# A second gating cycle that takes two of the second layer's four tiles in three passes

## The chip, the cores and the metric

The kernel runs on one core of a Trainium2 chip. The metric is the device time of one execution in microseconds (us); lower is better. The engines that matter here are TensorE (PE, with its weight loads shown apart as PEld), VectorE (DVE), ScalarE (ACT), GpSimd (POOL) and SyncE (SP), which issues transfers. Each engine works through its own list of instructions in the order written; between engines there are semaphores.

## The reference

One block of a gated cross-attention network, for 4 sequences of 1024 tokens of width 512, in float32. First x + tanh(g) * attention(layernorm(x), ctx) with 16 heads, a mask and an added matrix. Then the part that the change touches:

```python
def _coupling_net(h, w1, b1, w2, b2, w3, b3, w4, b4):
    h = _gelu(h @ w1 + b1)      # 512 -> 512
    h = _gelu(h @ w2 + b2)      # 512 -> 256
    h = _gelu(h @ w3 + b3)      # 256 -> 128
    return jax.nn.sigmoid(h @ w4 + b4)   # 128 -> 1
...
out = x                          # x is the layernorm of the first part's result
for _ in range(3):
    tf = _coupling_net(out, ...)
    combined = 0.7 * gf + 0.3 * tf
    coupling = BASE_COUPLING + adaptive_range * (combined - 0.5) * 2.0
    out = out + coupling * _twist(out)
```

`_twist` swaps and negates the four quarters of a row, so after any number of cycles `out` is alpha * x + beta * twist(x) with two numbers alpha and beta per token. The first layer is linear before its bias, so the kernel computes A = x @ w1 and B = twist(x) @ w1 once, and each cycle's first layer is gelu(alpha * A + beta * B + b1), an element-wise mix.

## The kernel before

The kernel has three phases: projections (up to about 300 us), attention (to about 1286 us) and the feed-forward phase, in `ffn_phase`, from there to the end. The change lies in the last alone.

`ffn_phase` goes through 4 batches (one sequence each, some 120 us), every batch through two column blocks j = 0 and 1 of 512 tokens. A batch projects the attention's output, normalises, computes A and B (`first_layer`), and then runs CYCLES = 3 gating cycles n = 0, 1, 2 on each block; the loop counter is k = 2n + j. All arrays lie transposed: 128 partitions by 4 tiles (m or t = 0 to 3) of features, 512 tokens along each row. For each (n, j):

- DVE, `mix(b, n, j)` for n = 1 and 2: multiplies and adds A and B into the tiles u[j][:, m] (f_u). For n = 1 that is one multiplication and one addition a tile. `coefficients` ahead of it turns the gate (f_coef) into alpha and beta.
- ACT, `h1`: Gelu of a tile of u, in place. It then raises h1_ready.
- PE, `layer2`: for each tile t, two matmuls (one for each half of the 256 outputs) of w2[:, t] with u[j][:, t], accumulated in f_acc.
- ACT `h2_half` twice, PE `layer3` (two matmuls), ACT `h3_all`, PE `layer4` (one matmul), ACT `gate` (a tanh), then DVE again for the other cycle.

A matmul has two forms. In plain float32 it is one `pe.matmul`, which the trace shows as two records. In the other form both operands are split into a high part of reduced precision (fp32r) and the rest as a low part; `three_pass` multiplies high by high, low by high and high by low, three records of a line each (L164, L165, L166). Cycle n = 0 has this form for all four tiles: ACT writes a second Gelu with an fp32r output (u_hi) ahead of the float32 one, and DVE subtracts the two into u_lo (`split_u`, L1624), which lies in the same place as u. Cycles 1 and 2 use plain float32 (L1328).

The order of the work is written out by hand. On PE, around one k: `layer2(k, tiles 1 to 3)`, `layer3(k)`, `layer2(k + 1, tile 0)`, `layer4(k)`. On ACT, the Gelus of the following cycle's tiles for the other block lie between the steps of k: h2_half, h2_half, h1 of tile 0, h3_all, h1 of tile 1, gate, h1 of tiles 2 and 3. So the h1 of block j in cycle n stands in the step k of the other block just ahead.

Two transfers for the following batch wait for the last use of u_hi, since they land in its memory or beside it: SP's `load_x(b + 1, 1)` into f_x_rows1 and POOL's `load_attention(b + 1, 0, part)` into X_hi and X_lo. Both count z2_ready up to cycle SPLIT - 1, so to the end of the second layer of cycle 0.

Of the kernel before, what the change touches and what calls it, by code (L numbers as in the profile page):

```python
# [10 lines left out]
F32 = mybir.dt.float32  # L11
F32R = mybir.dt.float32r
I32 = mybir.dt.int32
ALU = mybir.AluOpType
# [976 lines left out]
def ffn_phase(nc, weighted, x_bo, x_bo_stored, small, ident, wo_hi, wo_lo, w1_raw, w1_loaded, X_hi, X_lo, X_loaded, x1, x_loaded,  # L991
# [1 line left out]
    NJ = S // CH  # L993
    F2, F3 = E // 2, E // 4
    CYCLES = 3
    SPLIT = 1
    GPB = H // HPG
    LATE = 2 * (B * GPB - 2)

# [5 lines left out]
    with ExitStack() as ctx:  # L1005
# [127 lines left out]
        def turn(b, n, j):  # L1133

            return (CYCLES * b + n) * NJ + j

        def turn_split(b, n, j):

            return (SPLIT * b + n) * NJ + j

        def coef_steps(b, n, j):

# [101 lines left out]
        def _(pe):  # L1244
# [62 lines left out]
            def layer2(b, n, j, tiles):  # L1307

                k = turn(b, n, j)
                if n == 0 and 0 in tiles:  # L1310
                    if j == 0:
                        pe.wait_ge(own_read, 2 * ET * NJ * (b + 1))
                    else:
                        pe.wait_ge(shared_read, 4 * ET * NJ * (b + 1))
                for t in tiles:
                    if n < SPLIT:
                        pe.wait_ge(w2_lo_ready, b + 1)
                        pe.wait_ge(u_lo_ready, ET * turn_split(b, n, j) + t + 1)
                        for m in range(2):
                            ms = slice(m * P, (m + 1) * P)  # L1320
                            last = three_pass(pe, acc[:, 2 * j + m, :], w2_hi[:, t, ms], w2_lo[:, t, ms], u_hi[j][:, t, :], u_lo[j][:, t, :],
                                              t == 0, t == ET - 1)
                            if t == ET - 1:
                                last.then_inc(z2_ready, 1)
                        continue
                    pe.wait_ge(h1_ready, ET * k + t + 1)
                    for m in range(2):
                        last = pe.matmul(acc[:, 2 * j + m, :], w2[:, t, m * P:(m + 1) * P], u[j][:, t, :], start=t == 0, stop=t == ET - 1)  # L1328
                        if t == ET - 1:
                            last.then_inc(z2_ready, 1)  # L1330
# [75 lines left out]
        def _(act):  # L1406
# [51 lines left out]
            def h1(b, n, j, m):  # L1458
                k = ((CYCLES - 1) * b + n - 1) * NJ + j
                act.wait_ge(u_ready, ET * k + m + 1)  # L1460
                if n < SPLIT:
                    act.activation(u_hi[j][:, m, :], u[j][:, m, :], ACT.Gelu, bias=small.b1[:, m:m + 1])
                act.activation(u[j][:, m, :], u[j][:, m, :], ACT.Gelu, bias=small.b1[:, m:m + 1]).then_inc(h1_ready, 1)  # L1463

# [96 lines left out]
        def _(dve):  # L1561
# [55 lines left out]
            def split_w2(b):  # L1617
                dve.wait_ge(w2_hi_ready, b + 1)
                dve.tensor_tensor(w2_lo[:], w2[:], w2_hi[:].bitcast(F32), ALU.subtract).then_inc(w2_lo_ready, 1)

            def split_u(b, n, j):
                for m in range(ET):
                    dve.wait_ge(h1_ready, ET * turn(b, n, j) + m + 1)
                    dve.tensor_tensor(u_lo[j][:, m, :], u[j][:, m, :], u_hi[j][:, m, :].bitcast(F32), ALU.subtract).then_inc(u_lo_ready, 1)  # L1624

            def coefficients(b, n, j):

# [15 lines left out]
            def mix(b, n, j):  # L1643

                k = ET * (((CYCLES - 1) * b + n - 1) * NJ + j)
                dve.wait_ge(coef_step, coef_steps(b, n - 1, j))

                def multiply(m):
                    if n == 1:
                        dve.tensor_tensor(u[j][:, m, :], Bt[j][:, m, :], beta[:, j, :], ALU.mult).then_inc(mul_ready, 1)  # L1650
                    else:
                        dve.tensor_tensor(u[j][:, m, :], A[j][:, m, :], alpha[:, j, :], ALU.mult).then_inc(mul_ready, 1)
                        dve.tensor_tensor(Bt[j][:, m, :], Bt[j][:, m, :], beta[:, j, :], ALU.mult).then_inc(B_scaled, 1)

                def add(m):
                    dve.wait_ge(mul_ready, k + m + 1)
                    if n == 2:
                        dve.wait_ge(B_scaled, ET * (NJ * b + j) + m + 1)
                    other = A if n == 1 else Bt
                    dve.tensor_tensor(u[j][:, m, :], u[j][:, m, :], other[j][:, m, :], ALU.add).then_inc(u_ready, 1)  # L1660

                multiply(0)
                for m in range(1, ET):
                    multiply(m)
                    add(m - 1)
                add(ET - 1)

            def gated_columns(b, j):
# [45 lines left out]
            def batch(b, first, more):  # L1714
# [39 lines left out]
                for k in range(NJ * CYCLES):  # L1754
                    n, j = k // NJ, k % NJ
                    if n < CYCLES - 1:
                        coefficients(b, n, j)
                        mix(b, n + 1, j)
                        if n + 1 < SPLIT:
                            split_u(b, n + 1, j)  # L1760
                    else:
                        gated_columns(b, j)
                        y_columns(b, j)
                        if j == 0:
                            for s in range(TT):
                                finish(b, 0, s)
# [87 lines left out]
```

## Time and profile before

| what | value |
|---|---|
| median of 3 runs | 1780.76 us (1780.32 to 1783.08) |
| the profiled execution: its time | 1781.25 us |
| the profiled execution: its span | 1779.5 us |
| PE busy | 1744.4 us, 98% |
| DVE busy | 1467.6 us, 82% |
| ACT busy | 1250.7 us, 70% |
| POOL busy | 658.9 us, 37% |
| mean granted clock of TensorE | 0.994 |

The span runs from the first instruction to the last; the execution's own time holds 1.75 us more. In rows of the trace a start is in us from the span's start, and "x12" says that the row merges 12 like records. A record's duration on PE, DVE or ACT is longer than the distance to the next start, because instructions overlap in the pipeline: what an engine spends on one is read from the distance between starts.

### The profile page before, as it was taken

The page shows a single profiled execution, that of the slowest core. Times are in us where ns is not written, and L with a number is a line of the kernel's source. Part 1 is how long each engine was busy: PE and PEld are TensorE (multiplying, and loading weights), DVE is VectorE, ACT ScalarE, POOL GpSimd, SP SyncE. Part 2 cuts the span into 40 slices and gives each one's busy share as a digit, 9 for nine tenths or more (in the row PEclk, how much of TensorE's full clock was granted, in tenths as well). Part 3 has the DMA queues.
Part 4 walks back from the last instruction along what each step waited for, and adds up shares of the span by engine and source line. Part 5 has one row for each costly group of instructions (what it writes and reads, how often), then busy time and mean ns, then how long its engine had stood idle before and what let it go on. Part 6 is the DMA issues. An engine that isn't in the chain of part 4 may idle for free. (4 is left out here: it accounts for less than half of the span.)

```text
span 1779.5 us, 34050 instructions
## 1 busy us (share of the span) xinstructions
PE 1744.4 (98%) x12392; PEld 1290.0 (72%) x12392; DVE 1467.6 (82%) x2554; ACT 1250.7 (70%) x2185; POOL 658.9 (37%) x591
## 2 busy tenths in 40 slices
PE   7999999999999999999999999999999999999997
PEld 6888887777777777777777777777676585674873
DVE  5544545999999999999999999999777976877868
ACT  3232324999999999999999999999764365465455
POOL 3342342323278542487432695353325010010100
PEclk9999999999999999999999999999999999999999
DMA  7778675756367665377753676744512614212101
GB/s 266 254 247 287 230 265 153 181 159 144 107 170 202 125 145 120 106 215 159 145 134 85 185 190 125 159 97 114 158 51 71 192 48 118 86 54 66 63 1 48
DMA packets 152214, 254.63 MB, mean 143 GB/s; under 512 B 17024, under 2 KB 69504, under 8 KB 152064
## 3 DMA queue, kind: packets, MB, share of 16 engines
q1 hardware_dynamic: 101408, 157.73, 27.5%
q0 software_dynamic: 50080, 93.87, 23.8%
q8 instruction: 92, 1.51, 0.4%
q10 hardware_dynamic: 576, 1.05, 0.2%
q14 instruction: 58, 0.48, 0.1%
HBM read 168.44 MB, written 84.15 MB: 142 GB/s over the span
## 5 line engine op out<-in xcount | busy, mean ns | idle before, releaser
L967 DVE CUSTOM_DVE_ANT_0 a_neg<-a_sc_ps,am 128x1024 f32<-128x1024 f32 x512 | 620.9, 1213 | 1.3 <-PE a_sc_ps L820 1.3
L916 ACT ACTIVATE a_prob<-a_neg,a_row_min 128x1024 f32<-128x1024 f32 x512 | 586.0, 1144 | 7.7 <-DVE a_row_min L967 4.6
L832 PEld LDWEIGHTS a_tr_ps<-ident,a_prob 128*128 128x128 f32 x4096 | 460.3, 140 | 136.2 <-issue 100.3
L832 PE MATMUL a_tr_ps<-ident,a_prob 128*128 128x128 f32 x4096 | 545.8, 276 | 1.4 <-ACT a_probT L896 1.4
L942 DVE COPY a_probT<-a_tr_ps 128x512 f32<-128x512 f32 x512 | 353.8, 691 | 49.0 <-PE a_tr_ps L832 36.5
L896 ACT ACTIVATE a_probT<-a_tr_ps 128x512 f32<-128x512 f32 x512 | 305.6, 597 | 74.3 <-PE a_tr_ps L832 49.2
L716 POOL DMA_DIRECT2D a_q_st<-q_parts x144 | 79.6, 559 | 211.7 <-PE a_sc_ps L820 176.6
L853 PE MATMUL a_o_ps<-a_probT,v_first 128*32 128x256 f32 x2048 | 137.0, 385 | 0.0
L853 PE MATMUL a_o_ps<-a_probT,a_v 128*32 128x256 f32 x2048 | 136.4, 385 | 0.2 <-ACT a_probT L896 0.2
L1328 PE MATMUL f_acc<-f_u,f_w 128*128 128x512 f32 x256 | 115.9, 595 | 0.4 <-ACT f_u L1463 0.3
L820 PE MATMUL a_sc_ps<-k_first,a_q_st 96*128 96x512 f32 x384 | 113.7, 417 | 0.0
L820 PE MATMUL a_sc_ps<-a_k_st,a_q_st 96*128 96x512 f32 x384 | 113.1, 416 | 0.0
L916 ACT ACTIVATION_READ_ACCUMULATOR a_prob<-a_neg,a_row_min 128x1 f32 x512 | 97.0, 190 | 0.0
L721 POOL TENSOR_SCALAR a_m_raw<-a_m_raw 128x1024 f32<-128x1024 int32 x24 | 86.9, 3630 | 25.6 <-DMA a_m_raw<-mask 25.4
L1328 PEld LDWEIGHTS f_acc<-f_u,f_w 128*128 128x128 f32 x256 | 47.6, 190 | 61.4 <-issue 48.3
L853 PEld LDWEIGHTS a_o_ps<-a_probT,a_v 128*32 128x32 f32 x2048 | 53.7, 109 | 43.6 <-issue 20.6
L853 PEld LDWEIGHTS a_o_ps<-a_probT,v_first 128*32 128x32 f32 x2048 | 53.4, 109 | 43.3 <-issue 21.3
L132 POOL TENSOR_TENSOR st_o<-st_o,st_rinv 128x512 f32<-128x512 f32 x32 | 41.4, 1294 | 111.0 <-DMA st_rinv<-rinv_all 110.9
L820 PEld LDWEIGHTS a_sc_ps<-k_first,a_q_st 96*128 96x128 f32 x384 | 64.8, 189 | 9.4 <-DVE a_row_min L967 1.2
L820 PEld LDWEIGHTS a_sc_ps<-a_k_st,a_q_st 96*128 96x128 f32 x384 | 65.1, 189 | 8.5
L1222 POOL TENSOR_TENSOR f_rstd<-f_var_eps,f_minus_half 128x4 f32<-128x4 f32 x8 | 10.4, 1298 | 161.6 <-DVE f_neg_mean L1592 161.6
L463 DVE SCALAR_TENSOR_TENSOR p_out_lo<-p_acc,p_bias_k,p_out_hi 128x512 fp32r<-128x512 f32 x32 | 23.7, 749 | 55.1 <-ACT p_out_hi L395 55.1
(221 smaller groups left out, 3109.7 us busy)
## 6 DMA issues: line engine op xcount, KB each, us to landing
a_q_st<-q_parts POOLq DMA_DIRECT2D x144, 128.0 KB, 2.9
k_first<-k_parts POOLq DMA_DIRECT2D x24, 512.0 KB, 8.2
a_k_st<-k_parts POOLq DMA_DIRECT2D x24, 512.0 KB, 7.5
a_m_raw<-mask SPq DMA_DIRECT2D x24, 512.0 KB, 4.9
a_adj_raw<-adj SPq DMA_DIRECT2D x24, 512.0 KB, 6.1
p_x_raw<-x POOLq DMA_DIRECT2D x8, 1024.0 KB, 8.0
k_parts<-p_out_hi SPq DMA_DIRECT2D x32, 256.0 KB, 3.0
k_parts<-p_out_lo SPq DMA_DIRECT2D x32, 256.0 KB, 6.2
```

The lines of the kernel that those rows point to most:

```text
L132: pool.tensor_tensor(w.o[:], w.o[:], w.rinv[:], ALU.mult).then_inc(w.step, 1)
L463: dve.scalar_tensor_tensor(out_lo[:, m, :], acc[:, (n0 + m) % 4, :], bias[:, m:m + 1], out_hi[:, m, :].bitcast(F32), ALU.add, ALU.subtract ...
L716: pool.dma_start(q_st[qb][quad * D:(quad + 1) * D], src).then_inc(q_loaded[qb], 16)
L721: pool.tensor_scalar(m_raw[:, t % 2, :].bitcast(F32), m_raw[:, t % 2, :], 0.0, -BIG, ALU.is_equal, ALU.mult).then_inc(big_ready, 1)
L820: last = pe.matmul(sc_ps[:, r % 2, half * 512:(half + 1) * 512], q_st[qb][0:STACK, h, qt * P:(qt + 1) * P], k_st[par][0:STACK, h, half * 5 ...
L832: last = pe.transpose(tr_ps[:, half, j * P:(j + 1) * P], prob[:, r % NPROB, t * P:(t + 1) * P], ident[:])
L853: last = pe.matmul(o_ps[h * D:(h + 1) * D, prev % 2, 0:QB], v_sb[vpar][:, t, h * D:(h + 1) * D], probT[:, prev % 2, h, t, :], start=(t == ...
L896: act.activation(probT[:, (r // UB) % 2, h, 0:4, qt * P:(qt + 1) * P], tr_ps[:, 0, :].rearrange("p (t q) -> p t q", t=4), ACT.Copy).then_i ...
L916: act.activation(prob[:, r % NPROB, :], neg[:, r % 2, :], ACT.Exp, scale=-1.0, bias=row_min[:, r % 2:r % 2 + 1], accum_out=row_sum[:, r // ...
L942: dve.tensor_copy(probT[:, (r // UB) % 2, h, 4:8, qt * P:(qt + 1) * P], tr_ps[:, 1, :].rearrange("p (t q) -> p t q", t=4)).then_inc(tr_rea ...
L967: dve.tensor_tensor_reduce(out=neg[:, r % 2, :], in0=sc_ps[:, r % 2, :], in1=am[:, 2 * qb + qt, :], scale=-1.0, scalar=3.4e38, op0=ALU.add ...
L1328: last = pe.matmul(acc[:, 2 * j + m, :], w2[:, t, m * P:(m + 1) * P], u[j][:, t, :], start=t == 0, stop=t == ET - 1)
```

## The change

The second gating cycle (n = 1) takes its tiles 0 and 1 in three passes; tiles 2 and 3 stay float32. ACT's `h1` writes u_hi too for those two. DVE subtracts inside `mix`: the subtraction for tile 0 after the addition of tile 1, that for tile 1 after the addition of tile 2. SPLIT is 2 now, so the two transfers wait for the second layer of cycle 1.

```diff
-    SPLIT = 1
+    SPLIT = 2
+    PARTS = (4, 2)
...
-        def turn_split(b, n, j):
+        def parts_before(b, n, j):
 
-            return (SPLIT * b + n) * NJ + j
+            return NJ * sum(PARTS) * b + NJ * sum(PARTS[:n]) + PARTS[n] * j
...
                 for t in tiles:
-                    if n < SPLIT:
+                    if n < SPLIT and t < PARTS[n]:
                         pe.wait_ge(w2_lo_ready, b + 1)
-                        pe.wait_ge(u_lo_ready, ET * turn_split(b, n, j) + t + 1)
+                        pe.wait_ge(u_lo_ready, parts_before(b, n, j) + t + 1)
...
                 act.wait_ge(u_ready, ET * k + m + 1)
-                if n < SPLIT:
+                if n < SPLIT and m < PARTS[n]:
                     act.activation(u_hi[j][:, m, :], u[j][:, m, :], ACT.Gelu, bias=small.b1[:, m:m + 1])
...
+            def split_u_tile(b, n, j, m):
+                dve.wait_ge(h1_ready, ET * turn(b, n, j) + m + 1)
+                dve.tensor_tensor(u_lo[j][:, m, :], u[j][:, m, :], u_hi[j][:, m, :].bitcast(F32), ALU.subtract).then_inc(u_lo_ready, 1)
+
             def split_u(b, n, j):
-                for m in range(ET):
...
+                for m in range(PARTS[n]):
+                    split_u_tile(b, n, j, m)
...
                 for m in range(1, ET):
                     multiply(m)
                     add(m - 1)
+                    if n == 1 and m >= 2:
+                        split_u_tile(b, 1, j, m - 2)
                 add(ET - 1)
...
                         mix(b, n + 1, j)
-                        if n + 1 < SPLIT:
-                            split_u(b, n + 1, j)
```

On DVE, in the first batch, the mixing of block 0 for cycle 1 (f_u_18572 is u of block 0, f_u_lo_18574 and f_u_hi_18560 its low and high parts). Before:

```order
L1650 TENSOR_TENSOR f_u_18572<-f_B_18570,f_beta 128x512 [waits f_coef_step]
L1650 TENSOR_TENSOR f_u_18572<-f_B_18570,f_beta 128x512
L1660 TENSOR_TENSOR f_u_18572<-f_u_18572,f_A_18569 128x512 [waits f_mul_ready]
L1650 TENSOR_TENSOR f_u_18572<-f_B_18570,f_beta 128x512
L1660 TENSOR_TENSOR f_u_18572<-f_u_18572,f_A_18569 128x512 [waits f_mul_ready]
L1650 TENSOR_TENSOR f_u_18572<-f_B_18570,f_beta 128x512
L1660 TENSOR_TENSOR f_u_18572<-f_u_18572,f_A_18569 128x512 [waits f_mul_ready] x2
```

The same place on DVE in the changed kernel (its lines are numbered four on):

```order
L1654 TENSOR_TENSOR f_u_18572<-f_B_18570,f_beta 128x512 [waits f_coef_step]
L1654 TENSOR_TENSOR f_u_18572<-f_B_18570,f_beta 128x512
L1664 TENSOR_TENSOR f_u_18572<-f_u_18572,f_A_18569 128x512 [waits f_mul_ready]
L1654 TENSOR_TENSOR f_u_18572<-f_B_18570,f_beta 128x512
L1664 TENSOR_TENSOR f_u_18572<-f_u_18572,f_A_18569 128x512 [waits f_mul_ready]
L1624 TENSOR_TENSOR f_u_lo_18574<-f_u_18572,f_u_hi_18560 128x512 [waits f_h1_ready]
L1654 TENSOR_TENSOR f_u_18572<-f_B_18570,f_beta 128x512
L1664 TENSOR_TENSOR f_u_18572<-f_u_18572,f_A_18569 128x512 [waits f_mul_ready]
L1624 TENSOR_TENSOR f_u_lo_18574<-f_u_18572,f_u_hi_18560 128x512 [waits f_h1_ready]
L1664 TENSOR_TENSOR f_u_18572<-f_u_18572,f_A_18569 128x512 [waits f_mul_ready]
```

The two subtractions (L1624) are new; the last multiplication and the last two additions stand behind one or both of them.

On ACT, the same stretch: the step of cycle 0, block 1, with the Gelus of cycle 1, block 0 in it. Before:

```order
L1467 ACTIVATE f_h_1_18577<-f_acc,small_b_71 128x512 [waits f_z2_ready] x2
L1463 ACTIVATE f_u_18572<-f_u_18572,small_b_70 128x512 [waits f_u_ready]
L1471 ACTIVATE f_h_1_18577<-f_tr,small_b_72 128x512 [waits f_z3_ready]
L1463 ACTIVATE f_u_18572<-f_u_18572,small_b_70 128x512 [waits f_u_ready]
L1476 ACTIVATE f_coef<-f_z,small_half_b_75 128x512 [waits f_z4_ready]
L1463 ACTIVATE f_u_18572<-f_u_18572,small_b_70 128x512 [waits f_u_ready] x2
```

The same place on ACT in the changed kernel:

```order
L1468 ACTIVATE f_h_1_18577<-f_acc,small_b_71 128x512 [waits f_z2_ready] x2
L1463 ACTIVATE f_u_hi_18560<-f_u_18572,small_b_70 128x512 [waits f_u_ready]
L1464 ACTIVATE f_u_18572<-f_u_18572,small_b_70 128x512
L1472 ACTIVATE f_h_1_18577<-f_tr,small_b_72 128x512 [waits f_z3_ready]
L1463 ACTIVATE f_u_hi_18560<-f_u_18572,small_b_70 128x512 [waits f_u_ready]
L1464 ACTIVATE f_u_18572<-f_u_18572,small_b_70 128x512
L1477 ACTIVATE f_coef<-f_z,small_half_b_75 128x512 [waits f_z4_ready]
L1464 ACTIVATE f_u_18572<-f_u_18572,small_b_70 128x512 [waits f_u_ready] x2
```

A Gelu into f_u_hi stands ahead of the plain one for tiles 0 and 1; both still stand behind the two h2 halves.

## Rows read from the trace of the kernel before

**Rows 1.** The page, part 1: busy time, share of the span, instructions.
```profile
PE 1744.4 (98%) x12392; PEld 1290.0 (72%) x12392; DVE 1467.6 (82%) x2554; ACT 1250.7 (70%) x2185; POOL 658.9 (37%) x591
```
**Rows 2.** Chain of waits, second batch: start, us, engine, what, line.
```profile
1489.46 1.72 PE f_acc L1328 x4
...
1529.63 1.04 PE f_tr L1350 x8
```
**Rows 3.** Timeline of PE, second batch: start, us, engine, line, operation, out<-in, count.
```profile
1489.30 1.88 PE L1328 MATMUL f_acc<-f_u,f_w 128*128 128x512 f32 x4
1491.01 1.02 PE L1344 MATMUL f_z<-f_h,small_w 128*128 128x512 f32 x2
1491.87 5.31 PE L1328 MATMUL f_acc<-f_u,f_w 128*128 128x512 f32 x12
...
1498.92 1.88 PE L1328 MATMUL f_acc<-f_u,f_w 128*128 128x512 f32 x4
```
**Rows 4.** Timeline of ACT, second batch; in brackets idle time and its releaser.
```profile
1486.73 1.37 ACT L1467 ACTIVATE f_h<-f_acc,small_b 128x512 f32<-128x512 f32 x2 [2.75 <-PE f_acc L166]
1488.00 0.71 ACT L1463 ACTIVATE f_u<-f_u,small_b 128x512 f32<-128x512 f32 x1
1489.50 0.69 ACT L1471 ACTIVATE f_h<-f_tr,small_b 128x512 f32<-128x512 f32 x1 [0.79 <-PE f_tr L1336]
...
1492.66 1.32 ACT L1463 ACTIVATE f_u<-f_u,small_b 128x512 f32<-128x512 f32 x2
...
1497.81 0.71 ACT L1463 ACTIVATE f_u<-f_u,small_b 128x512 f32<-128x512 f32 x1
```
**Rows 5.** Timeline of DVE, second batch.
```profile
1485.81 0.68 DVE L1660 TENSOR_TENSOR f_u<-f_u,f_A 128x512 f32<-128x512 f32 x1
...
1502.42 0.55 DVE L1636 TENSOR_SCALAR f_coef<-f_coef,small_range,f_base 128x512 f32<-128x512 f32 x1 [4.14 <-ACT f_coef L1476]
```
**Rows 6.** Chain of waits, second batch: PE released by a subtraction of DVE.
```profile
1433.76 0.70 DVE X_lo L1604
1434.50 0.50 PE f_acc L164
```
**Rows 7.** Timeline of PE, second batch: two records of an unbroken three-pass stretch, then one behind rows 6.
```profile
1410.03 0.40 PE L166 MATMUL f_acc<-wo_lo,X_hi 128*128 128x512 f32 x1
...
1428.43 0.39 PE L166 MATMUL f_acc<-wo_lo,X_hi 128*128 128x512 f32 x1
...
1434.84 0.39 PE L165 MATMUL f_acc<-X_hi,f_w_lo 128*128 128x512 f32 x1
```
**Rows 8.** Timeline of PE's weight loads, second batch.
```profile
1493.42 0.36 PEld L1328 LDWEIGHTS f_acc<-f_u,f_w 128*128 128x128 f32 x2 [0.50 <-ACT f_u L1463]
```
**Rows 9.** Timeline of ACT, first batch.
```profile
1366.89 0.72 ACT L1463 ACTIVATE f_u<-f_u,small_b 128x512 f32<-128x512 f32 x1 [0.69 <-DVE f_u L1660]
```
**Rows 10.** Timeline of DVE, first batch.
```profile
1377.90 1.75 DVE L1660 TENSOR_TENSOR f_u<-f_u,w_raw 128x512 f32<-128x512 f32 x1
```
**Rows 11.** Timeline of POOL, first batch.
```profile
1377.50 1.60 POOL L141 TENSOR_TENSOR st_lo<-st_o,st_hi 128x512 f32<-128x512 f32 x1
```
**Rows 12.** Timeline of PE, first batch.
```profile
1369.48 1.02 PE L1344 MATMUL f_z<-f_h,small_w 128*128 128x512 f32 x2
...
1379.11 1.02 PE L1344 MATMUL f_z<-f_h,small_w 128*128 128x512 f32 x2
1380.46 5.42 PE L1328 MATMUL f_acc<-f_u,f_w 128*128 128x512 f32 x12 [0.33 <-ACT f_u L1463]
```
**Rows 13.** Stretches: us, busy of PE, PEld, DVE, ACT, POOL (x instructions), PEclk (granted clock), DMA, GB/s.
```profile
1350.00:1380.00 30.00, 27.75 (x85) 15.16 (x83) 24.08 (x27) 12.39 (x21) 17.75 (x15) 1.00 0.23 71
...
1460.00:1479.00 19.00, 18.92 (x81) 15.20 (x80) 13.52 (x22) 9.76 (x19) 1.56 (x2) 0.94 0.24 67
```
**Rows 14.** Timeline of POOL, second batch: a transfer is issued for the following one.
```profile
1487.67 0.74 POOL L1205 DMA_DIRECT2D X_hi<-att_parts  x1 [12.58 <-PE f_acc L166]
```
**Rows 15.** Issues of transfers: out<-in, queue, count, KB each, median us from issue to landing.
```profile
X_lo<-att_parts POOLq DMA_DIRECT2D x6, 1024.0 KB, 8.4
```

More of the change, by code:

```diff
@@ L1619, in split_w2 @@
                 dve.tensor_tensor(w2_lo[:], w2[:], w2_hi[:].bitcast(F32), ALU.subtract).then_inc(w2_lo_ready, 1)
+            def split_u_tile(b, n, j, m):
+                dve.wait_ge(h1_ready, ET * turn(b, n, j) + m + 1)
+                dve.tensor_tensor(u_lo[j][:, m, :], u[j][:, m, :], u_hi[j][:, m, :].bitcast(F32), ALU.subtract).then_inc(u_lo_ready, 1)
             def split_u(b, n, j):
-                for m in range(ET):
-                    dve.wait_ge(h1_ready, ET * turn(b, n, j) + m + 1)
-                    dve.tensor_tensor(u_lo[j][:, m, :], u[j][:, m, :], u_hi[j][:, m, :].bitcast(F32), ALU.subtract).then_inc(u_lo_ready, 1)
+                for m in range(PARTS[n]):
+                    split_u_tile(b, n, j, m)
             def coefficients(b, n, j):
```

## The prediction

> **What bounds the kernel now.** I read the busy shares first: PE is busy 98% of the span [rows 1], so what PE spends counts unless something makes it wait. Then the chain of waits, which shows whose waits set the end: in the gating cycles of the second batch every link from 1489.46 to 1529.63 is a matmul [rows 2], and the third and fourth batches repeat that pattern. Last the timelines of that stretch, engine by engine, since the change adds links between engines to a chain that holds only PE. A full PE there does not say that the others have room: it says that they are just in time, and how closely is the question.
>
> **What PE saves.** A float32 matmul takes 0.86 us: the four records of tile 0 start at 1489.30 and layer 4 follows at 1491.01, and layer 4, one matmul, ends as tile 1 starts at 1491.87 [rows 3]. In a three-pass stretch 81 records lie between the starts 1410.03 and 1428.43, 0.227 us each [rows 7], so 0.68 us a matmul. A tile is two matmuls: 1.72 before, 1.36 after, 0.36 saved. There are 4 batches x 2 blocks x 2 tiles: 16 x 0.36 = 5.8 us, if nothing waits.
>
> **What ACT and DVE add.** ACT gets 16 Gelus at a distance of 0.61 us (two in 1.32, one in 0.71 [rows 4]). DVE gets 16 subtractions with two inputs in SBUF, as the additions have, 0.68 long at a distance of about 0.60 (I take the addition's 0.68 [rows 5]). By amount both fit: DVE stands idle 4.14 us ahead of the coefficients of cycle 1 [rows 5]. By place they don't.
>
> **Tile 0, block 0 (k = 2).** The mixed tile is ready at 1485.81 + 0.68 = 1486.49 [rows 5], but ACT's first Gelu on it stands behind the two h2 halves and starts at 1488.00 [rows 4]. Before, it ended at 1488.71 and PE started tile 0 at 1489.30 with 0.59 in hand [rows 3]. Now the high part comes first, the plain one starts 0.61 later and ends at 1489.32. Only then can DVE subtract, 1489.35 to 1490.03; its queue holds nothing else until then, since three multiplications and two additions are through. PE's start behind a subtraction: the one that ended at 1434.46 let PE go at 1434.50, and the next record stood at 1434.84 instead of one distance later, so the steady pace began at 1434.61, 0.15 behind DVE's end [rows 6, 7]. Tile 0 thus runs at pace from 1490.18 and ends at 1491.54, against 1491.01 before. Stall 0.88, saving 0.36 (with rounding): layer 4 is 0.53 late. h3_all, at 1489.50 before [rows 4], is not late, since ACT is free at 1489.22.
>
> **Tile 1.** ACT goes h3_all, high part 1490.09, plain 1490.7 to 1491.4; DVE, having done the last multiplication and the third addition, subtracts 1491.43 to 1492.11. PE wants tile 1 when layer 4 is through, at 1491.87 + 0.53 = 1492.40: no stall, with about 0.1 to spare for the weights. The fourth addition, behind that subtraction, ends at 1492.7, in time for ACT's last Gelu. PE is through tile 1 at 1493.77.
>
> **Tile 2, where the second saving goes.** Its Gelu stands behind the gate, which waits for layer 4. Before, it started at 1492.66 and ended at about 1493.37; the weight load of tile 2 waited for it until 1493.42 [rows 4, 8], only 0.17 ahead of PE's turn at 1491.87 + 1.72 = 1493.59. This chain (layer 4, gate, Gelu, load) is measured from layer 4, not from tile 1. A tile 1 that is 0.36 shorter leaves PE waiting 0.36 longer: tile 2 starts 0.53 late, as layer 4 was. So the saving of tile 1 is nothing, and k = 2 ends 0.53 late.
>
> **Block 1 (k = 3).** The same, with one difference: the second h2 half comes later there, so the Gelu of tile 0 starts 1.11 ahead of PE's turn (1497.81, 1498.92 [rows 3, 4]) instead of 1.30 (1488.00, 1489.30). Plain Gelu to 1499.13, subtraction to 1499.84, pace from 1499.99, end 1501.35 against 1498.92 + 1.72 = 1500.64: 0.71 more. Tile 1's saving goes as before. Together 0.53 + 0.71 = 1.24 us a batch.
>
> **Cycle 2.** Its mixing starts when the gate of k = 2's step has come, 1502.42 [rows 5]; DVE waits for it, so it moves by the same 1.24, and so do ACT and PE behind it. Nothing is won back: cycle 2 had no PE stall to absorb. Three batches: 3.7 us.
>
> **The first batch.** GpSimd is still at work on the attention's output there, and DVE is late. At k = 2 the first Gelu starts at 1366.89 [rows 9], so the plain one ends at 1368.2, the subtraction at 1368.93, tile 0 at 1368.93 + 0.15 + 1.36 = 1370.44 against 1369.48 [rows 12]: 0.97. At k = 3 DVE's mixing before is slowed to one operation of 1.75 us for each of GpSimd's of 1.60 [rows 10, 11], until GpSimd ends at 1379.10; the addition of tile 1 ends at 1379.65, and the new subtraction of tile 0 stands behind it. DVE's start is 0.97 later there, but what it gets is one operation behind each GpSimd one, so I let that addition end where it did: subtraction 1379.6 to 1380.3, tile 0 at pace from 1380.4 to 1381.8, layer 4 to 1382.6, tile 1 to 1384.0, tile 2 (0.48 + 0.61 + 0.61 + about 0.05 behind layer 4) at 1384.3. Before, tile 1 started at 1380.46, already 0.33 late [rows 12], and tile 2 at 1382.28. That makes 2.1 us for this batch, and 1.2 if the mixing weren't slowed, 3.8 if it lost one slot of 1.75.
> The Trainium skill (SBUF — State Buffer, section "SBUF: two separate sides") has the shared port pair as an exclusive lock held for a whole instruction. That agrees with the 1.75 beside 1.60 [rows 10, 11]. By it the late start is swallowed, as I assume; by a proportional slowdown the mixing would keep its 0.97 and this batch would cost up to 0.9 more.
>
> **Transfers.** POOL issued the part for the next batch at 1487.67, at the end of the second layer of cycle 0, and the median to landing is 8.4 us [rows 14, 15]. Now it waits for cycle 1's, near 1508, and lands near 1518; PE needs it at 1530.7 [rows 2]. SP's load of f_x_rows1 moves to about 1498 and is needed later still. Behind POOL's waiting issue stands nothing before the next batch, behind SP's the store of y(b, 0), which isn't ready until 1530. Cost nothing; without that cover project would start late by the whole lack.
>
> **Sum.** 3.7 + 2.1 = 5.8 us. On the profiled execution's 1781.25 (span 1779.5 and 1.75 around it) that is 1787.1; that execution is 0.5 over the median of 1780.76, which the forecast starts from: 1786.6 us, slower by 0.33%. From both sides: the new wait of PE on DVE is measured on one row, 0.15; between 0 and 0.35 it moves the sum by -1.2 to +1.6. The first batch gives -0.9 to +1.7. Its own range is 1784.5 to 1789.
>
> **Rivals.**
> First, PE's saving counts and the waits don't: low parts are there when PE comes. Then 5.8 us come off: 1775.0. It decides at tile 0: the subtraction would have to end before 1489.2, 0.8 earlier than I find, so ACT would have to begin at 1487.2, while it is on the h2 halves from 1486.73 [rows 4]. For it speaks only that tile 0 was mixed 1.5 us before its Gelu. 7%.
> Second, tile 2 isn't tied to layer 4: the load row [rows 8] was merely the load's own turn, and tile 1's 0.36 is kept. Then a batch costs 0.53, the first about 1.4, together 3.0: 1783.8, within what a measurement can tell from no change (0.2%, 3.6 us). Against it, the row names ACT's Gelu as the releaser, 0.05 behind its end. 13%.
> Third, the clock. PE gets eight more gaps of 0.9 to 2.4 us. The granted clock fell to 0.94 over 19 us with PE busy 18.92, some 1.1 us, and stayed at 1.00 over 30 us with 2.25 idle [rows 13]. If each gap brought such a fall (stretches at 1.2 GHz between those at 2.4), 8 x 1.1 = 9: 1796. 8%.
> The Trainium skill speaks for it (TensorE: Matmul & The Clock Gate, section "A second HAM failure mode: psum-queue depth-cycling"): frequent short idles between groups of matmuls make the clock swing. The 1.00 over 2.25 us of idle [rows 13] is against that here.
> That the change doesn't do what it says is no rival: the orders of DVE and ACT show the new instructions where they should stand.
>
> **Chances.** The forecast 72%, so slower by over 0.2% (the forecast and the clock) 80%, within 0.2% 13%, faster 7%. Range: 1782 to 1790 takes in the second rival and the bounds of the first batch; outside lie the first and third (15%) and a little of the forecast's edges.
>
> **What would show it.** Right: in cycle 1 PE idles some 0.9 to 1.1 us ahead of L164 on f_u_hi, released by DVE's f_u_lo, eight times (over 2 once in the first batch), and 0.3 to 0.4 ahead of the first L1328 behind, released by ACT's f_u; batches two to four are 1.2 us longer. Wrong: no idle behind tile 1, project waiting for X_hi, or a granted clock under 0.98 between 1480 and 1530.

## The result and the profile after

The changed kernel takes 1788.6 us (median of 9 runs, 1785.08 to 1794.89) against 1782.17 us for the kernel before, run beside it (median of 9, 1780.32 to 1783.36). The ratio is 1.0041, with a 95% interval of 1.0032 to 1.0050: slower by 7.3 us (5.7 to 8.9). The forecast was 5.8 us more and 1786.6 us, with a range of 1782 to 1790. The profiled execution took 1789.46 us with a span of 1787.7 us, 8.2 us over the span before.

The page's first part after, with the same columns as [rows 1]:

```profile
PE 1745.3 (98%) x12424; PEld 1297.1 (73%) x12424; DVE 1477.2 (83%) x2570; ACT 1260.3 (71%) x2201; POOL 658.5 (37%) x591
```

PE's share of busy time reads 98% before and after, and its busy time even rose by 0.9 us, although the new matmuls are the shorter ones. The loss shows only in what isn't busy: span less busy time is 35.1 us before and 42.4 us after. ACT and DVE show their 16 new instructions each, 9.6 us.

The timeline of PE in the second batch shows it. Columns are start, us, engine, line, operation, operands, count; in brackets the idle time ahead and its releaser. Line 1337 is layer 3, 1345 layer 4, 1329 the float32 matmul:

```profile
1490.03 1.98 PE L1337 MATMUL f_tr<-f_h,f_w 128*128 128x512 f32 x4
1492.74 0.47 PE L164 MATMUL f_acc<-f_u_hi,f_w_hi 128*128 128x512 f32 x1 [0.73 <-DVE f_u_lo L1624]
...
1494.19 1.02 PE L1345 MATMUL f_z<-f_h,small_w 128*128 128x512 f32 x2
...
1496.60 3.70 PE L1329 MATMUL f_acc<-f_u,f_w 128*128 128x512 f32 x8
1500.21 1.98 PE L1337 MATMUL f_tr<-f_h,f_w 128*128 128x512 f32 x4
1503.11 0.47 PE L164 MATMUL f_acc<-f_u_hi,f_w_hi 128*128 128x512 f32 x1 [0.91 <-DVE f_u_lo L1624]
...
1504.55 1.02 PE L1345 MATMUL f_z<-f_h,small_w 128*128 128x512 f32 x2
```

Before, this stretch ran without a gap [rows 3]. The bracketed 0.73 is counted from the modelled end of layer 3's last record; from layer 3's start at 1490.03 tile 0 used to begin 1.83 us later, at 1491.86, so its first record is 0.88 late.

ACT and DVE at the same place, the rows that answer to [rows 4, 5]:

```profile
1489.29 1.37 ACT L1468 ACTIVATE f_h<-f_acc,small_b 128x512 f32<-128x512 f32 x2 [2.75 <-PE f_acc L166]
1490.55 0.71 ACT L1463 ACTIVATE f_u_hi<-f_u,small_b 128x512 fp32r<-128x512 f32 x1
1491.16 0.71 ACT L1464 ACTIVATE f_u<-f_u,small_b 128x512 f32<-128x512 f32 x1
```

```profile
1489.56 0.69 DVE L1664 TENSOR_TENSOR f_u<-f_u,f_A 128x512 f32<-128x512 f32 x1
1491.90 0.69 DVE L1624 TENSOR_TENSOR f_u_lo<-f_u,f_u_hi 128x512 fp32r<-128x512 f32 x1 [1.66 <-ACT f_u L1464]
```

The plain Gelu ends at 1491.87, DVE subtracts from 1491.90 to 1492.59, and PE starts at 1492.74. PE's next record stands at 1493.05, so it is at pace from 1492.82, 0.23 behind DVE's end and 0.96 late; the forecast had 0.15 and 0.88, from [rows 6, 7]. DVE idled 1.66 us: nothing else in its order could go ahead of the subtraction.

The weight loads of PE ahead of tile 2, the row that answers to [rows 8]:

```profile
1496.59 0.30 PEld L1329 LDWEIGHTS f_acc<-f_u,f_w 128*128 128x128 f32 x2 [0.44 <-ACT f_u L1464]
```

PE's last record of tile 1 starts at 1496.19 and is through at pace at 1496.42, so this load at 1496.59 has nothing left to hide behind. Before, it ran under a matmul.

Most readings below use one distance, taken from PE's timelines: from the start of layer 3 at k = 1 (cycle 0, block 1) to the first layer-4 matmul in columns of the last cycle, which spans everything the change touches in one batch. In us, from one profile each:

| kernel | first batch | second | third | fourth |
|---|---|---|---|---|
| before | 34.11 | 33.26 | 33.27 | 33.25 |
| changed | 35.90 | 34.61 | 34.63 | 34.65 |
| difference | +1.79 | +1.35 | +1.36 | +1.40 |

The four differences make 5.9 us. The rest of the 8.2 us lies outside that stretch, where the two kernels have the same instructions, and is the granted clock, less 0.9 us by which the phase began earlier. The stretches here have the columns of [rows 13]:

```profile
1462.00:1466.00 4.00, 4.00 (x12) 3.20 (x11) 1.23 (x1) 1.51 (x3) 0.00 (x0) 0.59 0.00 0
...
1702.00:1706.00 4.00, 4.00 (x23) 3.57 (x23) 2.21 (x5) 1.93 (x4) 0.00 (x0) 0.78 0.02 6
1706.00:1710.00 4.00, 4.00 (x16) 3.17 (x15) 1.48 (x2) 1.65 (x3) 0.00 (x0) 0.79 0.00 0
```

Each such fall costs about 1.6 us: from the last cycle to layer 3 of the next batch's k = 1 the profiles have 86.2 us or 87.8 us and nothing between. The kernel before had one of these (87.79 between its first and second batch), the changed one two (87.75 and 87.79), and one more in its first batch, between 1334 and 1340. These falls stand in the first layer, before the change's part of the batch, and follow 16 matmuls with one column of output; they are not where the new gaps are.

### The profile page after: what moved, and what is told of

Same layout as the page of the kernel before. It is cut to its first block and busy times, and to the rows that moved or that the text cites. A ratio compares the mean times of both kernels' runs of the same rounds, so it can differ in the third digit from the quotient of the medians.

```text
span 1787.7 us, 34162 instructions
## 1 busy us (share of the span) xinstructions
PE 1745.3 (98%) x12424; PEld 1297.1 (73%) x12424; DVE 1477.2 (83%) x2570; ACT 1260.3 (71%) x2201; POOL 658.5 (37%) x591
## 5 line engine op out<-in xcount | busy, mean ns | idle before, releaser
L1329 PE MATMUL f_acc<-f_u,f_w 128*128 128x512 f32 x192 | 87.9, 600 | 0.0
L1616 DVE TENSOR_TENSOR f_B<-f_B,f_acc 128x512 f32<-128x512 f32 x64 | 43.7, 683 | 31.6 <-PE f_acc L166 21.7
L380 ACT ACTIVATE p_c_hi<-p_c_raw 128x2048 fp32r<-128x2048 f32 x7 | 13.4, 1919 | 78.3 <-PE p_acc L166 50.4
```

## The experiments

All ratios are against the kernel before, run on the same chip in the same rounds; microseconds over or under before are the ratio's distance from 1, times 1782.

**Tile 0 alone.** In cycle 1 only tile 0 is taken in three passes.

```diff
-    PARTS = (4, 2)
+    PARTS = (4, 1)
...
-                    if n == 1 and m >= 2:
+                    if n == 1 and m == 2:
```

> Only tile 0 of cycle 1 is taken in three passes; tile 1 is float32 again, without its second Gelu and subtraction. Theory (the wait behind layer 4, gate and Gelu fixes when tile 2 starts, so tile 1's saving is worth nothing): as the changed kernel, 5.8 us over before (5.5 to 6.2), and no idle of PE ahead of tile 2. Rival (tile 1's saving of 0.36 counts, eight times): 2.9 us slower than the changed kernel, 8.7 over before.

Measured: 1787.4 us, ratio 1.0035 (1.0023 to 1.0048), 6.2 us over before. By distance a batch costs 34.70, 34.69 and 34.70 in the second to fourth, +1.43; the changed kernel +1.37. So tile 1's three passes, which are 0.36 us shorter, bring 0.06 a batch. Its first batch had 35.37 in this profile. In the trace layer 4 and what follows it are the same:

```profile
1489.76 0.47 PE L164 MATMUL f_acc<-f_u_hi,f_w_hi 128*128 128x512 f32 x1 [0.73 <-DVE f_u_lo L1624]
...
1491.21 1.02 PE L1345 MATMUL f_z<-f_h,small_w 128*128 128x512 f32 x2
1492.06 5.31 PE L1329 MATMUL f_acc<-f_u,f_w 128*128 128x512 f32 x12
1497.29 1.99 PE L1337 MATMUL f_tr<-f_h,f_w 128*128 128x512 f32 x4
```

From layer 4 to the next layer 3 it takes 6.08 us here with a float32 tile 1, and 1500.21 - 1494.19 = 6.02 us in the changed kernel with the shorter one. The saving of tile 1 is turned into the wait for tile 2, as the forecast had it; the rival that counted it is out.

**Late transfers alone.** The kernel before with the two waits for the next batch's transfers one cycle later.

```diff
-                            sp.wait_ge(z2_ready, 2 * turn(b, SPLIT - 1, 0) + 2)
+                            sp.wait_ge(z2_ready, 2 * turn(b, SPLIT, 0) + 2)
...
-                    pool.wait_ge(z2_ready, 2 * turn(b - 1, SPLIT - 1, 1) + 2)
+                    pool.wait_ge(z2_ready, 2 * turn(b - 1, SPLIT, 1) + 2)
```

> The kernel before, with only the two waits for transfers moved to the end of the second layer of cycle 1, as in the changed kernel. Theory (they are covered): 0 us, within 0.5. Rival (late transfers are the 1.5 us by which the changed kernel is over the forecast): +1.5 us.

Measured: 1781.35 us, ratio 0.9990 (0.9982 to 0.9999). The transfers are covered. In the changed kernel POOL issues at 1510.96 what it issued at 1487.67 before [rows 14], and PE needs it some 23 us later. The interval ends just under 1; its three later batches are 33.26, 33.25 and 33.26, as before. Its first batch had 33.25 where the kernel before had 34.11; further down such differences turn out to go with GpSimd's place.

**High passes first.** The changed kernel, but PE waits in cycle 1 for the high part only, does the four passes that read it, and then waits for the low part.

```diff
                     if n < SPLIT and t < PARTS[n]:
                         pe.wait_ge(w2_lo_ready, b + 1)
+                        if n == 1:
+                            pe.wait_ge(u_hi_ready, 2 * (NJ * b + j) + t + 1)
+                            for m in range(2):
+                                ms = slice(m * P, (m + 1) * P)
+                                pe.matmul(acc[:, 2 * j + m, :], w2_hi[:, t, ms], u_hi[j][:, t, :], start=t == 0, stop=False)
+                                pe.matmul(acc[:, 2 * j + m, :], w2_lo[:, t, ms], u_hi[j][:, t, :], start=False, stop=False)
+                            pe.wait_ge(u_lo_ready, parts_before(b, n, j) + t + 1)
+                            for m in range(2):
+                                pe.matmul(acc[:, 2 * j + m, :], w2_hi[:, t, m * P:(m + 1) * P], u_lo[j][:, t, :], start=False, stop=False)
+                            continue
...
-                    act.activation(u_hi[j][:, m, :], u[j][:, m, :], ACT.Gelu, bias=small.b1[:, m:m + 1])
+                    act.activation(u_hi[j][:, m, :], u[j][:, m, :], ACT.Gelu, bias=small.b1[:, m:m + 1]).then_inc(u_hi_ready, 1)
```

> The changed kernel, but in cycle 1 PE waits for the high part alone, does the four passes of a tile that read it, and only then waits for the low part and does the other two. Theory (the loss is PE's wait on the low part): that wait is covered by 4 x 0.227 = 0.91 us of passes; tile 0 then ends 0.36 earlier than in float32 on block 0 and 0.2 on block 1, 0.56 a batch in batches two to four, and in the first batch, where DVE's subtraction stands behind an addition held up by GpSimd, about 1.2 late: together -0.5 us against before (-1.5 to +0.5), 6 under the changed kernel. Rival (the added work on ACT and DVE costs by itself, wherever PE waits): no more than 1 us under the changed kernel.

Measured: 1781.37 us, ratio 0.9995 (0.9987 to 1.0004): 8 us under the changed kernel, with the same 16 Gelus and 16 subtractions. The batches are 32.71, 32.72 and 32.72, which is -0.55 each against the -0.56 worked out; the first is 36.12, +2.0 instead of +1.2, and it holds a fall of the clock (granted 0.50 from 1383 to 1386) behind 1.79 us in which PE idled. The wait is gone from the timeline:

```profile
1490.60 1.98 PE L1348 MATMUL f_tr<-f_h,f_w 128*128 128x512 f32 x4
1492.02 0.79 PE L1324 MATMUL f_acc<-f_u_hi,f_w_hi 128*128 128x512 f32 x1
...
1493.35 0.62 PE L1328 MATMUL f_acc<-f_u_lo,f_w_hi 128*128 128x512 f32 x2
1493.81 1.02 PE L1356 MATMUL f_z<-f_h,small_w 128*128 128x512 f32 x2
```

Layer 4 begins 3.21 us behind layer 3's start; 3.54 before, 4.16 in the changed kernel. The loss was the wait on the low part, not the work that makes it.

**Gelu of tile 2 ahead of the gate.** The changed kernel with one ACT instruction moved, in the step of cycle 0, block 1.

```diff
+                    if k == 1:
+                        h1(*other, 2)
                     if n < CYCLES - 1:
                         gate(b, n, j)
...
                     if between:
-                        h1(*other, 2)
+                        if k != 1:
+                            h1(*other, 2)
```

> The changed kernel, but in the step of cycle 0, block 1, ACT does the Gelu of tile 2 ahead of the gate instead of behind it. Theory (tile 2 waits on layer 4, gate, Gelu): PE's idle ahead of tile 2 of block 0 goes, 0.36 four times, 1.4 us under the changed kernel, 4.4 over before. Rival (that idle isn't there, or is made good by the next wait): as the changed kernel.

Measured: 1790.73 us, ratio 1.0041 (1.0029 to 1.0054), as the changed kernel. The whole time says no, the trace says yes and why. From layer 3 of k = 1 to that of k = 2 it is 9.94, 9.92 and 9.94 us in the three later batches against 10.18 in the changed kernel, 0.25 less where 0.36 was expected, and the load of tile 2 waits for nobody:

```profile
1499.62 0.19 PEld L166 LDWEIGHTS f_acc<-f_u_lo,f_w_hi 128*128 128x128 f32 x1
1499.85 0.42 PEld L1329 LDWEIGHTS f_acc<-f_u,f_w 128*128 128x128 f32 x2
```

The first batch takes it back: 37.52 us, where the changed kernel's profile had 35.90. PE idles 2.45 us ahead of tile 0 of block 1 there, and the granted clock is 0.50 from 1383 to 1386. The same gap was 2.18 us long in the changed kernel's profile, and no fall followed it. The moved Gelu needn't be the cause of the fall: the kernel with the first batch alone, further down, has the same one without it.

**The second Gelu alone.** The kernel before with late transfers, and ACT's Gelu into u_hi for tiles 0 and 1 of cycle 1, which nobody reads. DVE and PE are untouched.

```diff
-                if n < SPLIT:
+                if n == 1 and m < 2:
                     act.activation(u_hi[j][:, m, :], u[j][:, m, :], ACT.Gelu, bias=small.b1[:, m:m + 1])
```

> The kernel before with the later transfers and, in cycle 1, ACT's second Gelu for tiles 0 and 1, whose result nobody reads; DVE and PE work as before. Theory (what counts is how far tile 0's plain Gelu is from PE's turn, not ACT's idle time): PE waits 0.2 us more at tile 0 of block 0 and 0.4 at that of block 1, 0.6 a batch and about 1.0 in the first, together 2.8 us over before (2.0 to 3.5), near half of the changed kernel's loss. Rival (ACT is 70% busy, so 16 Gelus fit): 0 us.

Measured: 1784.5 us, ratio 1.0008 (0.9993 to 1.0022). The interval can't tell the theory from the rival, but the distances can: 33.80 in all four batches, +0.54 in the second to fourth (0.6 expected). The first has 33.80 too, where the kernel before had 34.11 in its profile; the 1.0 expected there didn't come. So 1.6 us of the later batches' 4.1 come with ACT's instruction alone, though ACT was busy only 70% of the span: in its order the plain Gelu moves 0.61 back.

**The passes alone.** The kernel before with late transfers; in cycle 1 PE takes tiles 0 and 1 in three passes, all on the high part left from cycle 0. The low part of cycle 1 is left out.

```diff
                     pe.wait_ge(h1_ready, ET * k + t + 1)
+                    if n == 1 and t < 2:
+                        for m in range(2):
+                            ms = slice(m * P, (m + 1) * P)
+                            three_pass(pe, acc[:, 2 * j + m, :], w2_hi[:, t, ms], w2_lo[:, t, ms], u_hi[j][:, t, :], u_hi[j][:, t, :], t == 0, False)
+                        continue
```

> The kernel before with the later transfers, and in cycle 1 PE takes tiles 0 and 1 in three passes, all three on the high part that cycle 0 left, waiting for the plain Gelu alone; ACT and DVE do nothing new. The low part of cycle 1 is left out. Theory: tile 0 gives its 0.36 us on both blocks, tile 1's is lost behind layer 4, gate and Gelu: 0.72 a batch, none in the first, where DVE is the limit: 2.2 us under before (1.5 to 2.8). Rival (all 32 matmuls' saving counts): 5.8 us under before.

Measured: 1779.33 us, ratio 0.9986 (0.9971 to 1.0002), 2.5 us under before where 2.2 was expected and the rival had 5.8; the interval excludes a gain of 5.8. The distances are 32.54 three times, -0.72 each, the figure worked out to the second digit. The first batch has 35.07, so nothing was gained there. Even with ACT and DVE spared, half of what PE saves is lost behind layer 4, gate and Gelu.

**The changed kernel again.**

> The changed kernel once more, beside the others on one chip. Theory (5.9 us of waits, and the rest of the 7.3 measured is the clock's scatter): 5.9 us over before at the same granted clock. Rival (the new gaps bring clock falls): a mean granted clock at least 0.001 under that of the kernel before, and 7.3 us or more.

Measured: 1790.95 us (12 runs, 1787.77 to 1793.94), ratio 1.0047 (1.0032 to 1.0062), 8.4 us. Its mean granted clock is 0.9916, against 0.9931 for 34 of the 35 executions of the kernel before beside it. The one left out (1796.13 us, clock 0.960) stands 12 us above all others; with it the mean is 0.9922, and the rival's condition on the clock isn't met. So the means point to the clock but don't settle it. The profile shows a place: its later batches are 34.65, 34.64 and 34.64, but the first takes 40.44 us, 6.3 more than before. PE there:

```profile
1363.93 1.98 PE L1337 MATMUL f_tr<-f_h,f_w 128*128 128x512 f32 x4
1369.51 0.77 PE L164 MATMUL f_acc<-f_u_hi,f_w_hi 128*128 128x512 f32 x1 [3.60 <-DVE f_u_lo L1624]
...
1372.21 1.91 PE L1345 MATMUL f_z<-f_h,small_w 128*128 128x512 f32 x2
```

DVE, and then POOL:

```profile
1364.74 1.75 DVE L1664 TENSOR_TENSOR f_u<-f_u,f_A 128x512 f32<-128x512 f32 x1
1366.41 1.75 DVE L1654 TENSOR_TENSOR f_u<-f_B,f_beta 128x512 f32<-128x512 f32 x1
1368.09 0.68 DVE L1664 TENSOR_TENSOR f_u<-f_u,f_A 128x512 f32<-128x512 f32 x1
1368.69 0.68 DVE L1624 TENSOR_TENSOR f_u_lo<-f_u,f_u_hi 128x512 fp32r<-128x512 f32 x1
```

```profile
1362.68 1.59 POOL L137 TENSOR_TENSOR st_hi<-st_lo,st_o 128x512 f32<-128x512 f32 x1
1364.35 1.59 POOL L139 TENSOR_TENSOR st_hi<-st_lo,st_hi 128x512 f32<-128x512 f32 x1
1366.02 1.59 POOL L141 TENSOR_TENSOR st_lo<-st_o,st_hi 128x512 f32<-128x512 f32 x1
```

GpSimd's group of five came 3.4 us before layer 3 here and so fell on the mixing of k = 2; in the kernel before it came 6.5 us before (1359.12) and was over 0.1 us behind layer 3's start. DVE's operations with two inputs in SBUF took 1.75 us each beside one of GpSimd's, and 0.68 without. The subtraction stands behind a run of them, PE idles 3.60 us, and towards the end of that gap the clock falls (stretches, columns as in [rows 13]):

```profile
1366.00:1369.00 3.00, 0.00 (x0) 0.00 (x0) 3.00 (x4) 2.11 (x4) 1.59 (x1) 0.89 0.18 66
1369.00:1373.00 4.00, 3.49 (x7) 2.48 (x8) 2.77 (x5) 1.13 (x2) 0.00 (x0) 0.50 0.70 212
1373.00:1375.00 2.00, 2.00 (x5) 1.23 (x4) 0.12 (x1) 0.84 (x2) 1.28 (x1) 0.50 0.00 1
```

A granted clock of 0.50 is the lower of the two levels, 1.2 GHz. Layer 4, at 1.02 otherwise, takes 1.91.

**Later batches alone, and the first batch alone.** The changed kernel's cycle 1 only where b > 0, and only where b is 0. In both the count of low parts is adapted.

```diff
-                    if n < SPLIT and t < PARTS[n]:
+                    if n == 0 or (b > 0 and n < SPLIT and t < PARTS[n]):
...
-                if n < SPLIT and m < PARTS[n]:
+                if b > 0 and n < SPLIT and m < PARTS[n]:
...
-                    if n == 1 and m >= 2:
+                    if b > 0 and n == 1 and m >= 2:
```

> The changed kernel's cycle 1 in batches two to four alone; the first batch as before. Theory (1.37 us a batch there, the same in every execution; what is over the forecast comes from the first batch, where GpSimd's place varies): 4.1 us over before, with no more scatter than before has (about 5 us from end to end). Rival (the excess comes from clock falls that the later batches' gaps bring): 5.5 us or more, and wide scatter.

> The changed kernel's cycle 1 in the first batch alone. Theory: between 1.8 us (as in the changed kernel's profile) and 6 (as in its second profile, where DVE's subtraction was 3.6 us late), on the mean some 3.4, with wide scatter. Rival (as forecast): 2.1 us and no scatter.

Measured: later batches alone 1787.5 us (7 runs, 1785.52 to 1788.81), ratio 1.0026 (1.0015 to 1.0038), 4.6 us; by distance 34.64, 34.66 and 34.64, so 4.2. The scatter of 3.3 us is as the theory had it, but the interval (2.7 to 6.8) doesn't exclude the rival's 5.5; the distances do, since no fall stands in them. The first batch alone 1786.03 us (11 runs, 1783.64 to 1788.05), ratio 1.0022 (1.0013 to 1.0031), 3.9 us. The two make 8.5, the whole change 7.3 and 8.4. The first batch costs about as much as the other three together, and the interval of 2.3 to 5.5 us excludes the forecast's 2.1. The expected wide scatter of the first batch didn't show: 4.4 us from end to end, less than the kernel before has.

By distance the changed first batch had 37.50 us in this profile, 1.60 more than in the first profile of the changed kernel. GpSimd isn't the reason, since its group stands in the same place (8.1 us ahead of layer 3 in both) and so does the gap of PE in block 1. The changed kernel, PE and one stretch:

```profile
1380.74 0.47 PE L164 MATMUL f_acc<-f_u_hi,f_w_hi 128*128 128x512 f32 x1 [2.18 <-DVE f_u_lo L1624]
1381.05 0.39 PE L165 MATMUL f_acc<-f_u_hi,f_w_lo 128*128 128x512 f32 x1
...
1376.00:1390.00 14.00, 11.82 (x32) 5.18 (x30) 12.77 (x20) 8.28 (x13) 4.83 (x6) 1.00 0.87 275
```

The first batch alone:

```profile
1381.55 0.76 PE L164 MATMUL f_acc<-f_u_hi,f_w_hi 128*128 128x512 f32 x1 [2.19 <-DVE f_u_lo L1624]
1382.12 0.63 PE L165 MATMUL f_acc<-f_u_hi,f_w_lo 128*128 128x512 f32 x1
...
1382.00:1384.00 2.00, 2.00 (x6) 1.52 (x6) 1.81 (x4) 0.48 (x1) 0.00 (x0) 0.50 1.13 364
1376.00:1390.00 14.00, 11.80 (x29) 6.03 (x28) 11.18 (x16) 6.54 (x11) 4.24 (x4) 0.88 0.81 248
```

It is a fall of the clock behind the new gap, and the 1.60 us are what it costs. All six kernels whose first batch has low parts in cycle 1, one profile each ("ahead" is from the start of GpSimd's group to that of layer 3):

| kernel | GpSimd ahead | longest gap of PE in cycle 1 | clock falls behind it | first batch |
|---|---|---|---|---|
| tile 0 alone | 8.0 | 1.57 | no | 35.37 |
| changed | 8.1 | 2.18 | no | 35.90 |
| high passes first | 8.0 | 1.79 | yes | 36.12 |
| first batch alone | 8.1 | 2.19 | yes | 37.50 |
| Gelu of tile 2 early | 7.7 | 2.45 | yes | 37.52 |
| changed, again | 3.4 | 3.60 | yes, twice as long | 40.44 |

In none of the other seven profiles does the clock fall in this part of the first batch. There the distance follows GpSimd's place: 33.25 and 33.27 at 7.7 and 7.6 us ahead (late transfers alone, and the first profile of the version below), 34.11 at 6.5 (before), 34.63 at 5.8 (the second profile of the version below) and 35.13 at 5.1 (later batches alone).

**A version that takes both lessons.** High passes first and the early Gelu of tile 2, in batches two to four; the first batch keeps float32 in cycle 1. Against the changed kernel, with the passes as in "High passes first":

```diff
-                    if n < SPLIT and t < PARTS[n]:
+                    if n == 0 or (b > 0 and n < SPLIT and t < PARTS[n]):
                         pe.wait_ge(w2_lo_ready, b + 1)
+                        if n == 1:
+                            pe.wait_ge(u_hi_ready, 2 * (NJ * (b - 1) + j) + t + 1)
...
+                    if b > 0 and k == 1:
+                        h1(*other, 2)
...
-                            h1(*other, 2)
+                        if not (b > 0 and k == 1):
+                            h1(*other, 2)
...
-                    if n == 1 and m >= 2:
+                    if b > 0 and n == 1 and m >= 2:
```

> Three passes in cycle 1 only in batches two to four, there with the high passes ahead of the wait for the low part and with the Gelu of tile 2 ahead of the gate in the step of cycle 0, block 1; the first batch as before. Theory: 0.55 a batch from the high passes and 0.26 from the early Gelu, measured singly, 0.8 x 3 = 2.4 us under before (1.5 to 3). Rival (the two don't add, or what they give is lost in cycle 2): 0 to 1 us.

> High passes first and the early Gelu, in batches two to four, once more for the interval: 2.4 us under before (1.5 to 3).

Measured: 1780.42 us, ratio 0.9987 (0.9973 to 1.0001), and again 1780.85 us, ratio 0.9995 (0.9986 to 1.0004): 2.3 and 0.9 us under before, neither clear of no change. By distance the three batches are 32.47, 32.46 and 32.47, -0.80 each, as the sum of the two parts said. The gain of 2.4 us is in the traces; that the kernel as a whole is faster than before isn't shown.

## Why the prediction was right, and which term was off

**PE's waits.** The direction and the mechanism were right, and in the later batches the steps came out in their places and nearly in their sizes. Tile 0 of block 0 made layer 4 late by 0.62 (0.53 forecast; k = 2 ends 0.55 late by layer 3), block 1 added 0.76 (0.71) and cycle 2 another 0.06 (none). A batch: 1.37 against 1.24, and three of them 4.1 against 3.7. The passes alone and the Gelu alone split it: -0.72 for PE's saving, +0.54 for ACT's place in the order. That leaves 1.55, by subtraction, for the link from ACT over DVE to PE. The high passes first took away 1.92, which is that link and, if the parts add, some of ACT's share. The start of PE behind DVE, 0.23 instead of 0.15 and twice a batch, is 0.16, the size of the 0.13 a batch by which I was low.

**Tile 2 is tied to layer 4.** Shown three times: by tile 0 alone (the shorter tile 1 is worth 0.06), by the passes alone (0.72 instead of 1.43), and by the early Gelu (0.25 back, not all of the 0.36).

**Transfers.** At nothing, as forecast.

**The first batch.** This is the term that was mis-sized: 2.1 us forecast, 1.79 in the first profile, but 3.9 us over 11 executions. Two things were left out of it. First, the fall of the clock. The forecast had PE idle "over 2 once in the first batch" and put no price on that gap, because it took the clock as a rival for all eight gaps or for none. The one long gap is where falls came: in four profiles with 1.8 to 2.5 us idle there, three had a fall of 1.6 us behind it. The mean granted clock of the first batch alone, 0.9920 against 0.9927, says the same with about 1.2 us of 1780 (an estimate; each execution's clock is on record to three digits).

Second, GpSimd's place. GpSimd starts when its own transfer lands, 8.1 us ahead of layer 3 in one profile of the changed kernel and 3.4 in the other, and I took 6.5, its place in the one profile of before, for its place in every execution. Where it was early, a changed first batch without a fall took 35.90 and an unchanged one 33.26, so the change costs 2.6 there and not 1.79; the kernel before had 0.86 more than these in its own profile, where GpSimd came later. Block 0, for which the forecast had 0.97, was only 0.26 late at that early place. These 2.6 and a fall of 1.6 in most executions would about make the 3.9 (an estimate from one profile each). Where GpSimd was late, PE waited 3.60 us. "I let that addition end where it did" holds for the early place: in the first profile tile 0 of block 1 is at pace 14.44 us behind layer 3, and the forecast had 14.8. How often GpSimd is late isn't known; the scatter of the first batch alone, less than that of before, speaks for seldom. That the forecast's upper bound for this batch, 3.8, came near the measured value is luck, since its reason, "if it lost one slot of 1.75", isn't what the profiles show.

**The total.** The later batches' 4.1 and the first batch's 3.9 make 8.0, where the forecast had 5.8; the first rounds gave 7.3 and the later ones 8.4. With 8.4 the median was 1790.95 us, just over the range's end of 1790. That 1788.6 lay inside owes something to which rounds were taken first.

**The clock.** The rival had eight falls, one for each new gap, 9 us. In the later batches the gaps of 0.73 and 0.91 are followed by no fall in any profile: the distances would show one. In the first batch the rival was right in four of six profiles. The forecast weighed it against [rows 13], and read those rows too kindly twice. The fall of "some 1.1 us" was cut by the stretch's start at 1460; whole it is 1.6. And the 2.25 us of idle at a clock of 1.00 were one execution: 2.05 of them stand ahead of 1357.14, before layer 3 of k = 0 in the first batch. Ten of the thirteen profiles have such a gap of 1.95 to 2.17 us there, and in three of them (the second Gelu alone, high passes first, Gelu of tile 2 early) a fall followed, granted 0.55 to 0.59 over 3 or 4 us with PE busy throughout. So a gap of 2 us brings a fall in some executions and not in others. The rest of the falls are the ones that the kernel before has too, at 1.6 us each. The mean granted clock is 0.9926 and 0.9916 for the changed kernel and 0.9930, 0.9931 (without the one execution named above) and 0.9927 for the one before. How much of that difference is falls behind the gaps of the first batch, and how much chance in the others, stays open.

The Trainium skill's rule weighed in the prediction (TensorE: Matmul & The Clock Gate, "A second HAM failure mode: psum-queue depth-cycling"), that frequent short idles between groups make the clock swing, isn't borne out by the gaps of 0.73 to 0.91 us here; the falls of the first batch came behind single gaps of 1.79 us and more. Its rule on the shared port pair, that DVE or GpSimd holds it for a whole instruction (SBUF — State Buffer, "SBUF: two separate sides"), is borne out, with 1.75 us of DVE beside 1.59 of GpSimd.

## What to carry to other kernels

Before cheaper work is put on a full engine, look at when the engines that feed it are done, not at how idle they are: ACT at 71% and DVE at 83% had time enough and no place for it. A saving survives only up to the next wait, so ask of each piece what fixes the start of the piece behind it. A long new gap on TensorE can cost more than its own length: price a fall of the clock for each such gap singly, and look for it in several profiles. When a product has a part that is ready early and one that is ready late, wait for each apart and let the early passes cover the late operand; and where an engine with its own rhythm shares a port, take its place from several profiles.

## What the runs showed of the hardware

- A matmul of 512 columns in float32 takes 0.86 us and one in three fp32r passes 0.68, at the full clock.
- Behind a subtraction of DVE that PE waits for, PE is at pace 0.23 us after the subtraction's end in the profile (1492.59 and 1492.82); in the first layer it was 0.15 (1434.46 and 1434.61).
- PE idle for 0.73 to 0.91 us, 1.44 us or 1.57 us was followed by no fall of the clock. Behind 1.8 to 2.5 us of idle the clock fell to 0.50 in some executions and stayed at 1.00 in others (2.19 us with a fall, 2.18 us without), which costs 1.6 us; around the end of 3.60 us of idle it fell to 0.50 for almost 7 us.
- A fall of the clock to 0.59 over 4 us with PE busy all the time followed 16 matmuls of one column, at the same place of a batch in several kernels, in some batches and not in others.
